# A three-layer graph attention kernel: transposes of h by DMA, attention rows in PSUM, the skip connection as an accumulating DMA

## The chip, the cores and the metric

The kernel runs on one core of one Trainium2 chip. The metric is the device time in microseconds (us) of one execution; one launch computes all 128 graphs.

## The reference, cut to what matters

The input x is [128 graphs, 128 nodes, 256 features] in float32, adj is [128, 128, 128] in int32. All weights are float32; there are three layers.

```python
h = relu(layernorm(x))                       # over the 256 features, no affine part
mask = adj + eye > 0
for l in range(3):
    si, sj = h @ attn_w[l, :256], h @ attn_w[l, 256:]
    scores = leaky_relu(si[:, :, None] + sj[:, None, :] + attn_b[l], slope 0.2)
    attn = softmax(where(mask, scores, -inf), axis=-1)
    agg = einsum('bij,bjd->bid', attn, h)
    h1 = layernorm(h + agg) * g1[l] + beta1[l]
    ff = gelu(h1 @ W1[l] + b1[l]) @ W2[l] + b2[l]      # 256 -> 1024 -> 256
    h = layernorm(h1 + ff) * g2[l] + beta2[l]
out = x + h
```

## The kernel before, in words

**Tiling.** Four graphs make a group (T = 4), nodes on the 128 partitions; there are 32 groups and so 96 items (a group in one layer). Items are numbered s: eight groups go through layer 0, then the same eight through layer 1, then layer 2, and then come the next eight, so that one round has 24 slots (PER = 24, RING = 8). Precision is kept with split operands: a float32 value becomes two float16 values, hi and lo, and each product is three matmuls (hi by hi, lo by hi, hi by lo).

**Stages of an item.** Dot products with the two attention vectors (L613, L616 on VectorE). s_j is spread over rows by TensorE (L404) into the PSUM bank p_att. Scores, row maxima (L631, L637). Leaky ReLU and exponentials on ScalarE (L507 to L513). The probabilities are transposed by TensorE (L410) into p_att again, split into hi and lo (L518, L660), and aggregate with the split X (L422). Residual, statistics (L650, L579, L584 to L587), the inverse deviation on GpSimd (L786, L788), normalization on ScalarE into norm1 (L488). norm1 is transposed by TensorE, 8 blocks of 128x128 in float32 (L432), and split into hT_hi (ScalarE, L534) and hT_lo (VectorE, L665). GpSimd makes the residual h_res (L798, L800). Then for each of eight chunks c of the hidden width: first product (L366), GELU and its split (L478, L483, L572), second product (L380), which adds up in PSUM. Residual of the feed-forward into res2 (L675, feed_residual), statistics, inverse deviation, norm2 (L812, norm_feed), layer output (L826, L828). In the last layer the input is added from a second copy, x_again, which SyncE has loaded (L835), and the result is stored.

**Order.** There is no planner. Each engine runs a function slot(r, s), written out by hand, that interleaves parts of up to eight items; within it the chunks c = 0 to 7 order everything. In slot s TensorE, VectorE and ScalarE work on the chunks of item s. At c = 0 TensorE aggregates for item s + 1, at c = 4 it transposes norm1 of s + 1 and spreads s_j of s + 2, at c = 7 it transposes the probabilities of s + 2. VectorE does feed_residual of item s - 1 at c = 2; this waits until norm2 of item s - 2 is complete, because res2 and norm2 have one buffer each:

```python
            def feed_residual(r, s):
                dve.wait_ge(ff_done, total(r, s, C, C))
                dve.wait_ge(h_res_steps, total(r, s, 2, 2))
                if later(r, s):
                    dve.wait_ge(norm2_ready, total(r, s - 1, 4, 4))
```

Every engine executes its own list in order, and semaphores tie the engines together. The two tensors p_pair (each two PSUM banks) are used in turn: item s gathers its second product in p_pair[s % 2], and before that the transposes of norm1 and the aggregate of s + 1 use the one that is free. All DMAs of before are issued by SyncE, in one queue.

Of the kernel before, what the change touches and what calls it, by code (L numbers as in the profile page):

```python
# [35 lines left out]
P = 128  # L36
B, N, D = 128, 128, 256
L = 3
# [15 lines left out]
FIRST_SLOT = -4  # L54
# [38 lines left out]
def x_total(r, s, n):  # L93

    v = 4 * s + RING * (s // PER) + max(0, s % PER - (PER - RING)) + n
    return (4 * PER + RING) * r + v if isinstance(r, int) else r * (4 * PER + RING) + v


def group_of(r, s):
    return RING * (r + s // PER) + s % RING  # L100

# [32 lines left out]
def gnn_kernel(nc, x, adj, attn_w, attn_b, W1, b1, W2, b2, g1, beta1, g2, beta2, out):  # L134
    with ExitStack() as ctx:
# [37 lines left out]
        x_again = [w2_f32[:, i * T:(i + 1) * T, :] for i in range(2)]  # L173
# [19 lines left out]
        hT_hi = [sb(f"hT_hi{i}", [P, KD, TN], F16) for i in range(2)]  # L193
        hT_lo = [sb(f"hT_lo{i}", [P, KD, TN], F16) for i in range(2)]
# [16 lines left out]
        p_att = ps("p_att", [P, T, N])  # L211

# [7 lines left out]
        def nT_banks(s):  # L220
            return p_pair[s % 2][:].rearrange("p (k u) d -> p k (u d)", k=KD)

        def agg_banks(s):
            return p_pair[(s - 1) % 2]

# [9 lines left out]
        x_again_loaded = [sem(f"x_again_loaded{i}") for i in range(2)]  # L235
        stored = [sem(f"stored{i}") for i in range(2)]
        mask_steps = sem("mask_steps")
        x0_ready = sem("x0_ready")
        dots_ready = sem("dots_ready")
# [15 lines left out]
        nT_psum = sem("nT_psum")  # L255
# [25 lines left out]
        def _(sp):  # L281
# [20 lines left out]
            def load_again(g):  # L302
                sp.dma_start(x_again[g % 2], graphs(x, g)).then_inc(x_again_loaded[g % 2], 16)

            def store(r, s):
                g = group_of(r, s)
                sp.wait_ge(x_steps, x_total(r, s, 5))
                sp.dma_start(graphs(out, g), y_out[g % 2]).then_inc(stored[g % 2], 16)
                if g + 2 < G:
                    load_again(g + 2)  # L310
            def slot(r, s):
                if is_item(r, s + 2) and layer_of(s + 2) == 0 and group_of(r, s + 2) + 2 < G:
                    sp.wait_ge(x0_ready, group_total(r, s + 2, 4, 4))
                    load_x(group_of(r, s + 2) + 2)
# [13 lines left out]
                if (r, s) == (0, 5):  # L328
                    sp.wait_ge(w_lo_ready, 4 * L)
                    load_again(0)  # L330
                    load_again(1)
# [21 lines left out]
        def _(pe):  # L353
            def hidden(r, s, c):

                l, i = layer_of(s), s % 2
                if c == 0:
                    pe.wait_ge(hT_hi_ready, total(r, s, 1, 1))
# [26 lines left out]
            def fold_bias(l):  # L385
# [3 lines left out]
                for c in range(C):  # L389
                    for k in range(KD):  # L390
                        mm = pe.matmul(p_att[:, 0, c:c + 1], w1_f32[:, k, c * P:(c + 1) * P], beta1_col[:, l, k:k + 1],
# [3 lines left out]
            def spread_sj(r, s):  # L395

                pe.wait_ge(dots_ready, total(r, s, 8, 8))
                if later(r, s):
                    pe.wait_ge(pT_lo_ready, total(r, s - 1, 1, 1))
                if isinstance(r, int) and r == 0 and s in FOLD_AT:  # L400
                    fold_bias(FOLD_AT[s])
                    pe.wait_ge(bias_ready, FOLD_AT[s] + 1)
                for t in range(T):
                    mm = pe.transpose(p_att[:, t, :], s_j[s % RING][:, t:t + 1].broadcast_to([P, P]), ident[:])  # L404
                mm.then_inc(sj_rows_ready, 1)

            def transpose_probs(r, s):
                pe.wait_ge(probs_ready, total(r, s, 4, 4))
                for t in range(T):
                    mm = pe.transpose(p_att[:, t, :], probs[:, t, :], ident[:])  # L410
                mm.then_inc(pT_psum, 1)

            def aggregate(r, s):
# [3 lines left out]
                if later(r, s):  # L417
                    pe.wait_ge(hT_lo_ready, total(r, s - 1, 1, 1))
# [6 lines left out]

            def transpose_norm1(r, s):
                if later(r, s, 2):
                    pe.wait_ge(res2_ready, total(r, s - 2, 2, 2))
                pe.wait_ge(norm1_ready, total(r, s, 4, 4))
                for k in range(KD):  # L430
                    for t in range(T):
                        mm = pe.transpose(nT_banks(s)[:, k, t * N:(t + 1) * N],  # L432
                                          norm1[:, t, k * P:(k + 1) * P], ident[:])
                mm.then_inc(nT_psum, 1)

            def slot(r, s):
                for c in range(C):
# [15 lines left out]
                    if c == 4 and is_item(r, s + 1):  # L453
                        transpose_norm1(r, s + 1)
# [9 lines left out]
        def _(act):  # L464
# [32 lines left out]
            def norm_attention(r, s):  # L497
                act.wait_ge(rstd_ready[1], total(r, s, 2, 2))
                if later(r, s):
                    act.wait_ge(nT_psum, total(r, s - 1, 1, 1))  # L500
# [15 lines left out]
            def copy_probs(r, s):  # L516
                act.wait_ge(pT_psum, total(r, s, 1, 1))
                act.activation(pT_hi[:], p_att[:].rearrange("p t n -> p (t n)"), ACT.Copy).then_inc(pT_hi_ready, 1)  # L518
# [10 lines left out]
            def high_hT(r, s):  # L529

                act.wait_ge(nT_psum, total(r, s, 1, 1))
                if later(r, s, 2):
                    act.wait_ge(hid_psum, total(r, s - 2, C, C))
                act.activation(hT_hi[s % 2][:], nT_banks(s), ACT.Copy).then_inc(hT_hi_ready, 1)  # L534

            def slot(r, s):
                if isinstance(r, int) and r == 0 and s in (0, 3):
                    act.wait_ge(bias_ready, 1 if s == 0 else L)
                for c in range(C):
# [6 lines left out]
                    if c == 3 and is_item(r, s + 2):  # L546
                        high_X(r, s + 2)
                    if c == 4 and is_item(r, s + 1):
                        high_hT(r, s + 1)
# [4 lines left out]
                    if c == 7 and is_item(r, s + 3) and layer_of(s + 3) == 0:  # L554
                        norm_input(r, s + 3)
# [4 lines left out]
        def _(dve):  # L560
# [44 lines left out]
            def dot_products(r, s, pair):  # L605

                l, q = layer_of(s), s % RING
                if l == 0:
# [3 lines left out]
                for t in (2 * pair, 2 * pair + 1):  # L612
                    dve.tensor_tensor_reduce(out=dots[:, 2 * t, :], in0=X[q][:, t, :], in1=attn_rows[:, l, 0, :], scale=1.0,  # L613
                                             scalar=attn_b_col[:, l:l + 1], op0=ALU.mult, op1=ALU.add,
                                             accum_out=s_i[q][:, t:t + 1]).then_inc(dots_ready, 1)
                    dve.tensor_tensor_reduce(out=dots[:, 2 * t + 1, :], in0=X[q][:, t, :], in1=attn_rows[:, l, 1, :], scale=1.0,  # L616
# [3 lines left out]
            def add_bias(l):  # L620
                dve.wait_ge(bias_psum, l + 1)
                dve.tensor_tensor(b1_eff[:, l, :], p_att[:, 0, 0:C], b1_col[:, l, :], ALU.add).then_inc(bias_ready, 1)

            def add_scores(r, s):
# [5 lines left out]
                for t in range(T):  # L630
                    dve.scalar_tensor_tensor(out=scores[:, t, :], in0=p_att[:, t, :], scalar=s_i[q][:, t:t + 1],  # L631
# [26 lines left out]
            def low_probs(r, s):  # L658
                dve.wait_ge(pT_hi_ready, total(r, s, 1, 1))
                dve.tensor_tensor(pT_lo[:], p_att[:].rearrange("p t n -> p (t n)"), pT_hi[:],  # L660
                                  ALU.subtract).then_inc(pT_lo_ready, 1)

            def split_hT(r, s):
                dve.wait_ge(hT_hi_ready, total(r, s, 1, 1))
                dve.tensor_tensor(hT_lo[s % 2][:], nT_banks(s), hT_hi[s % 2][:], ALU.subtract).then_inc(hT_lo_ready, 1)  # L665
# [17 lines left out]
            def last_output(r, s):  # L683
# [4 lines left out]
                dve.wait_ge(x_again_loaded[s % 2], 16 * G // 2)  # L688
# [8 lines left out]
                dve.wait_ge(x_steps, x_total(r, s, 4))  # L697
                dve.tensor_tensor(y, y, x_again[s % 2], ALU.add).then_inc(x_steps, 1)

            def slot(r, s):  # L700
                starts = is_item(r, s + 4) and layer_of(s + 4) == 0

                late = isinstance(r, int) and (r, s) == (0, -3)
                if isinstance(r, int) and (r, s) == (0, -2):
# [3 lines left out]
                for c in range(C):  # L708
# [5 lines left out]
                    if c == 6 and starts and not late:  # L714
                        dve.wait_ge(stat_steps[0], group_total(r, s + 4, 10, 4))
                    if isinstance(r, int) and (r, s, c) == (0, -2, 3):
# [12 lines left out]
                    if isinstance(r, int) and (r, s, c) == (0, -2, 2):  # L729
                        input_statistics(0, 1)  # L730
                    if isinstance(r, int) and (r, s, c) == (0, -2, 3):
                        aggregates(0, group_total(0, 1, 10, 8))
                    if c == 3 and is_item(r, s - 1):
                        feed_statistics(r, s - 1)
                    if c == 4 and isinstance(r, int) and r == 0 and s + 2 in FOLD_AT:
                        add_bias(FOLD_AT[s + 2])
# [5 lines left out]
                    if c == 5 and is_item(r, s + 1):  # L742
                        split_hT(r, s + 1)
                    if c == 5 and starts and not late:
                        input_statistics(r, s + 4)
                    if c == 6 and is_item(r, s + 2):
                        low_probs(r, s + 2)
                    if c == 6 and starts and not late:
                        aggregates(0, group_total(r, s + 4, 10, 8))
                    if c == 6 and is_item(r, s + 2):  # L750
                        row_sums(r, s + 2)
                    if c == 6 and starts:
# [15 lines left out]
        def _(pool):  # L768
# [21 lines left out]
            def h_residual(r, s):  # L790
# [3 lines left out]
                if is_item(r, s + 1):  # L794
                    pool.wait_ge(dots_ready, total(r, s + 1, 8, 8))
# [82 lines left out]
```

## Time and profile before

| quantity | value |
|---|---|
| median of 3 runs (lowest to highest) | 2402.95 us (2402.5 to 2403.74) |
| profiled execution: its own time | 2401.22 us |
| its span | 2399.4 us |
| mean granted TensorE clock | 0.995 of full speed |
| busy, TensorE matmul | 2333.0 us (97%), 16608 instructions |
| busy, VectorE | 1869.7 us (78%), 5974 instructions |
| busy, ScalarE | 1892.0 us (79%), 3498 instructions |
| busy, GpSimd | 1698.2 us (71%), 1543 instructions |
| the DMA queue of SyncE | 77184 packets, 67.79 MB, 9.1% of 16 engines' span |

The span runs from the first to the last instruction. The profiled execution lies 1.7 us below the median of the three runs. Busy time is the union of an engine's instructions. A matmul's end is modelled, so on TensorE the distance between starts says more than the durations: a 128x256 float16 matmul has 273 ns beside it, and they follow each other every 0.11 us.

### The profile page before, as it was taken

Reading aid. Unit: us, or ns where it says so; the run is one execution under the profiler, and the core shown is the slowest. Engines: PE = TensorE matmul, PEld = TensorE weight load, DVE = VectorE, ACT = ScalarE, POOL = GpSimd, SP = SyncE. Lnnn points to the kernel's source line nnn. Section 1 sums busy time; section 2 is a strip of 40 time slices with the busy share of each in tenths; the row PEclk is TensorE's granted clock in tenths of the full one; section 3 lists DMA queues with packets and bytes.
Section 4 is the critical chain, followed back from the end, with each engine's and each line's share of the span. In section 5 each row is a group of like instructions: output and inputs, shape, how many; then the busy total and the mean of one; then the engine's idle time right before and its main releaser. Section 6 shows DMA issues by size and latency. Waiting matters only on the chain.

```text
span 2399.4 us, 47629 instructions
## 1 busy us (share of the span) xinstructions
PE 2333.0 (97%) x16608; PEld 1649.3 (69%) x16608; DVE 1869.7 (78%) x5974; ACT 1892.0 (79%) x3498; POOL 1698.2 (71%) x1543
## 2 busy tenths in 40 slices
PE   3999999999999999999999999999999999999997
PEld 2667777776666777777666777777766677777775
DVE  6887777777888777777888787878788877787874
ACT  4878787878888878787888877778788887878783
POOL 3567676768887666667887767676878776767686
PEclk9999999999999999999999999999999999999998
DMA  5200000001211000001121000000121100000012
GB/s 162 87 28 27 1 1 2 1 19 41 93 62 36 1 1 1 1 1 36 54 78 60 23 2 1 1 1 2 53 67 63 41 2 1 1 1 1 19 42 65
DMA packets 77421, 70.83 MB, mean 30 GB/s; under 512 B 7040, under 2 KB 75648, under 8 KB 77184
## 3 DMA queue, kind: packets, MB, share of 16 engines
q1 hardware_dynamic: 77184, 67.79, 9.1%
q8 instruction: 134, 2.20, 0.4%
q14 instruction: 103, 0.84, 0.1%
HBM read 51.01 MB, written 16.78 MB: 28 GB/s over the span
## 4 chain that ended last, share of the span: by engine, by line
PE 66%; POOL 16%; DVE 11%; ACT 3%; issue 2%; POOLq 0%; DVEq 0%
PE p_pair L380 29%; PE p_hid L366 28%; PE p_pair L422 4%; PE p_pair L432 2%; POOL rstd L786 2%; DVE dots L613 2%; DVE g_lo L572 2%; POOL w_f L835 2%; POOL h_res L798 2%; POOL h_res L800 2%; POOL norm L812 2%; DVE res L675 2%; POOL w_f L828 2%; POOL X_lo L804 2%; POOL w_f L826 2%
## 5 line engine op out<-in xcount | busy, mean ns | idle before, releaser
L380 PE MATMUL p_pair<-w_hi,g_hi 128*128 128x256 f16 x3072 | 837.6, 273 | 0.0
L380 PE MATMUL p_pair<-w_lo,g_hi 128*128 128x256 f16 x3072 | 837.6, 273 | 0.0
L380 PE MATMUL p_pair<-w_hi,g_lo 128*128 128x256 f16 x3072 | 837.5, 273 | 0.0
L572 DVE TENSOR_TENSOR g_lo<-p_hid,g_hi 128x512 f16<-128x512 f32 x768 | 528.6, 688 | 396.2 <-ACT g_hi L483 389.7
L478 ACT ACTIVATE p_hid<-p_hid,b_eff 128x512 f32<-128x512 f32 x768 | 504.5, 657 | 316.9 <-PE p_hid L366 315.7
L798 POOL TENSOR_TENSOR h_res<-norm,g_rows 128x1024 f32<-128x1024 f32 x96 | 227.7, 2372 | 384.0 <-DVE res L675 377.3
L483 ACT ACTIVATE g_hi<-p_hid 128x512 f16<-128x512 f32 x768 | 458.6, 597 | 24.4
L366 PE MATMUL p_hid<-hT_hi,w_hi 128*128 128x512 f16 x1536 | 458.2, 380 | 1.5 <-DVE g_lo L572 1.4
L366 PE MATMUL p_hid<-hT_hi,w_lo 128*128 128x512 f16 x1536 | 458.3, 380 | 0.0
L366 PE MATMUL p_hid<-hT_lo,w_hi 128*128 128x512 f16 x1536 | 457.9, 380 | 0.0
L786 POOL TENSOR_TENSOR rstd<-var_eps,minus_half 128x4 f32<-128x4 f32 x224 | 242.2, 1081 | 259.0 <-DVE minus_mean L587 253.7
L380 PEld LDWEIGHTS p_pair<-w_lo,g_hi 128*128 128x128 f16 x3072 | 300.7, 98 | 106.5 <-issue 0.3
L380 PEld LDWEIGHTS p_pair<-w_hi,g_hi 128*128 128x128 f16 x3072 | 300.7, 98 | 105.6 <-issue 0.4
L380 PEld LDWEIGHTS p_pair<-w_hi,g_lo 128*128 128x128 f16 x3072 | 300.7, 98 | 34.8
L488 ACT ACTIVATE norm<-res,shift,rstd 128x256 f32<-128x256 f32 x384 | 199.4, 590 | 97.6 <-POOL shift L788 97.6
L366 PEld LDWEIGHTS p_hid<-hT_hi,w_lo 128*128 128x128 f16 x1536 | 150.6, 98 | 182.2 <-issue 1.7
L366 PEld LDWEIGHTS p_hid<-hT_lo,w_hi 128*128 128x128 f16 x1536 | 150.6, 98 | 182.2 <-issue 1.7
L579 DVE BATCH_NORM_STATS2 bn<-res 128x6 f32<-128x256 f32 x768 | 269.5, 416 | 3.3
L800 POOL TENSOR_TENSOR h_res<-h_res,res_rows 128x1024 f32<-128x1024 f32 x96 | 227.0, 2364 | 7.5
L812 POOL TENSOR_SCALAR norm<-res,rstd,shift 128x256 f32<-128x256 f32 x384 | 207.5, 555 | 10.0
L650 DVE SCALAR_TENSOR_TENSOR res<-p_pair,row_inv,X 128x256 f32<-128x256 f32 x384 | 159.1, 477 | 67.6 <-PE p_pair L422 67.5
L804 POOL TENSOR_TENSOR X_lo<-X,X_hi 128x1024 f16<-128x1024 f32 x96 | 204.6, 2132 | 0.0
(68 smaller groups left out, 3658.5 us busy)
## 6 DMA issues: line engine op xcount, KB each, us to landing
x_in<-in_x SPq DMA_DIRECT2D x32, 512.0 KB, 4.1
w_f<-in_x SPq DMA_DIRECT2D x32, 512.0 KB, 5.8
out<-w_f SPq DMA_DIRECT2D x32, 512.0 KB, 4.2
adj_in<-in_adj SPq DMA_DIRECT2D x32, 256.0 KB, 4.5
w_f<-in_L_gnn_W SPq DMA_DIRECT2D x6, 1024.0 KB, 6.1
attn_rows<-in_L_gnn_attn_w SPq DMA_DIRECT2D x1, 768.0 KB, 5.9
g_rows<-in_L_gnn_g SPq DMA_DIRECT2D x2, 384.0 KB, 7.5
b_rows<-in_L_gnn_b SPq DMA_DIRECT2D x1, 384.0 KB, 6.7
```

The costliest lines, as they stand in the source:

```text
L366: mm = pe.matmul(p_hid[in_ring(s, c, PF_RING)][:], w[l][:, k, cols], h[i][:, k, :], start=(n == 0), stop=(n == 3 * KD - 1))
L380: mm = pe.matmul(ff_banks(s)[:, t, :], g[i][:, nodes], w[l][:, c, :], start=(c == 0 and t % 2 == 0 and n == 0), stop=(c == C - 1 and n == ...
L478: act.activation(p_hid[k][:], p_hid[k][:], ACT.Gelu, bias=b1_eff[:, l, c:c + 1], scale=1.0 / WSCALE).then_inc(gelu_ready, 1)
L483: act.activation(g_hi[i][:], p_hid[k][:], ACT.Copy).then_inc(g_hi_ready, 1)
L488: act.activation(dst[:, t, :], src[:, t, :], func, bias=shift[n][s % 2][:, t:t + 1], scale=rstd[n][s % 2][:, t:t + 1]).then_inc(done, 1)
L572: dve.tensor_tensor(g_lo[i][:], p_hid[k][:], g_hi[i][:], ALU.subtract).then_inc(g_lo_ready, 1)
L579: dve.bn_stats(bn[n][:, t, :], src[:, t, :]).then_inc(stat_steps[n], 1)
L786: pool.tensor_tensor(rstd[n][s % 2][:], var_eps[n][:], minus_half[:], ALU.pow).then_inc(rstd_ready[n], 1)
L798: pool.tensor_tensor(h_res[i][:], norm1[:], rows(g1_rows, l, T), ALU.mult).then_inc(h_res_steps, 1)
L800: pool.tensor_tensor(h_res[i][:], h_res[i][:], rows(res_rows, l, T), ALU.add).then_inc(h_res_steps, 1)
L804: pool.tensor_tensor(X_lo[:], X[s % RING][:], X_hi[:], ALU.subtract).then_inc(X_lo_ready, 1)
L812: pool.tensor_scalar(norm2[:, t, :], res2[:, t, :], rstd[2][s % 2][:, t:t + 1], shift[2][s % 2][:, t:t + 1], ALU.mult, ALU.add).then_inc(n ...
```

## The change

1. **Transposes of h.** The eight float32 transposes of norm1 on TensorE (L432) go, and so do the two splits out of PSUM (L534, L665). In their place ScalarE copies norm1 to float16 (h_hi, high_h, at c = 3; high_X moves to c = 4), GpSimd subtracts (low_h, h_lo), and SyncE issues two DMA transposes SBUF to SBUF for each item, each of [128, 1024] float16 (turn_h). The first product reads hT in the order [t, k].
2. **GpSimd's order.** Before: inverse deviation of s + 1, h_residual of s + 1, low_X of s + 2, inverse deviation, norm_feed and (after the skip connection and the input's inverse deviation) layer_output of s - 1. After: inverse deviation of s + 1; inverse deviation, norm_feed and layer_output of s - 2; low_h of s + 1; low_X; h_residual; the input's inverse deviation; the skip connection of s - 2.
3. **Rows in PSUM.** p_att goes. s_j and the transposed probabilities use the two banks of the p_pair that the aggregate will use. The free bank takes the two attention vectors of a layer (p_rows), copied once for eight items by VectorE; the dot products read them there. They move from c = 1 (item s + 2) to c = 5 (item s + 3). The input's statistics move one slot earlier, to c = 1 and c = 2.
4. **Skip connection.** x_again, its loads and the additions (L835, L698) go. GpSimd issues a DMA from x that accumulates onto y_out, and the store waits for it.

The core of the diff (the changes of buffers' declarations, the prologue's slots and the renaming of banks are left out):

```diff
@@ sync @@
+            def turn_h(r, s):
+                i = s % 2
+                if later(r, s, 2):
+                    sp.wait_ge(hid_psum, total(r, s - 2, C, C))
+                for h, hT, made, turned in ((h_hi, hT_hi, h_hi_ready, hT_hi_ready), (h_lo, hT_lo, h_lo_ready, hT_lo_ready)):
+                    sp.wait_ge(made, total(r, s, 1, 1))
+                    sp.dma_start_transpose(hT[i][:].rearrange("p t k n -> p (t k) n"),
+                                           h[:].rearrange("p t d -> p (t d)")).then_inc(turned, 16)
...
                 if is_item(r, s - 3) and layer_of(s - 3) == L - 1:
                     store(r, s - 3)
+                if is_item(r, s + 1):
+                    turn_h(r, s + 1)
@@ tensor @@
                 if c == 0:
-                    pe.wait_ge(hT_hi_ready, total(r, s, 1, 1))
+                    pe.wait_ge(hT_hi_ready, total(r, s, 16, 16))
...
                     if c == 0 and n == 2 * KD:
-                        pe.wait_ge(hT_lo_ready, total(r, s, 1, 1))
-                    mm = pe.matmul(p_hid[in_ring(s, c, PF_RING)][:], w[l][:, k, cols], h[i][:, k, :],
+                        pe.wait_ge(hT_lo_ready, total(r, s, 16, 16))
+                    mm = pe.matmul(p_hid[in_ring(s, c, PF_RING)][:], w[l][:, k, cols], h[i][:, :, k, :],
                                    start=(n == 0), stop=(n == 3 * KD - 1))
...
             def spread_sj(r, s):
                 pe.wait_ge(dots_ready, total(r, s, 8, 8))
-                if later(r, s):
-                    pe.wait_ge(pT_lo_ready, total(r, s - 1, 1, 1))
+                if later(r, s, 3):
+                    pe.wait_ge(res2_ready, total(r, s - 3, 2, 2))
...
-                    if c == 4 and is_item(r, s + 1):
-                        transpose_norm1(r, s + 1)
@@ scalar @@
-            def high_hT(r, s):
-                act.wait_ge(nT_psum, total(r, s, 1, 1))
...
+            def high_h(r, s):
+                act.wait_ge(norm1_ready, total(r, s, 4, 4))
+                if later(r, s):
+                    act.wait_ge(hT_hi_ready, total(r, s - 1, 16, 16))
+                act.activation(h_hi[:], norm1[:], ACT.Copy).then_inc(h_hi_ready, 1)
@@ vector @@
+                if q == 0 and pair == 0:
+                    dve.tensor_copy(p_rows[:], attn_rows[:, l]).then_inc(rows_ready, 1)
+                    dve.wait_ge(rows_ready, rows_total(r, s))
...
-                    if c == 1 and is_item(r, s + 2):
-                        if is_item(r, s - 2):
-                            dve.wait_ge(x_steps, x_total(r, s - 2, 4))
-                        dot_products(r, s + 2, 0)
-                        dot_products(r, s + 2, 1)
...
+                    if c == 1 and starts and not late:
+                        input_statistics(r, s + 5)
+                    if c == 2 and starts and not late:
+                        aggregates(0, group_total(r, s + 5, 10, 8))
...
-                    if c == 5 and is_item(r, s + 1):
-                        split_hT(r, s + 1)
...
+                    if c == 5 and is_item(r, s + 3):
+                        dot_products(r, s + 3, 0)
+                        dot_products(r, s + 3, 1)
@@ gpsimd @@
             def h_residual(r, s):
                 pool.wait_ge(norm1_ready, total(r, s, 4, 4))
-                if is_item(r, s + 1):
-                    pool.wait_ge(dots_ready, total(r, s + 1, 8, 8))
...
+            def low_h(r, s):
+                pool.wait_ge(h_hi_ready, total(r, s, 1, 1))
+                if later(r, s):
+                    pool.wait_ge(hT_lo_ready, total(r, s - 1, 16, 16))
+                pool.tensor_tensor(h_lo[:], norm1[:], h_hi[:], ALU.subtract).then_inc(h_lo_ready, 1)
...
                 pool.wait_ge(x_steps, x_total(r, s, 4))
-                pool.wait_ge(x_again_loaded[i], lane_total(r, s - 2 * RING))
-                pool.tensor_tensor(y_out[i], y_out[i], x_again[i], ALU.add).then_inc(x_steps, 1)
+                g = group_of(r, s)
+                pool.dma_start(y_out[i], x.rearrange("(g t) n d -> n g t d", t=T)[:, g],
+                               accum_op=ALU.add).then_inc(skipped[i], 16)
...
                 if is_item(r, s + 1):
                     inverse_deviation(s + 1, 1, total(r, s + 1, 10, 10), total(r, s + 1, 2, 1))
-                    h_residual(r, s + 1)
+                if is_item(r, s - 2):
+                    inverse_deviation(s - 2, 2, total(r, s - 2, 10, 10), total(r, s - 2, 2, 1))
+                    norm_feed(r, s - 2)
+                    layer_output(r, s - 2)
+                if is_item(r, s + 1):
+                    low_h(r, s + 1)
                 if is_item(r, s + 2):
                     low_X(r, s + 2)
-                if is_item(r, s - 1):
-                    inverse_deviation(s - 1, 2, total(r, s - 1, 10, 10), total(r, s - 1, 2, 1))
-                    norm_feed(r, s - 1)
+                if is_item(r, s + 1):
+                    h_residual(r, s + 1)
+                if is_item(r, s + 5) and layer_of(s + 5) == 0:
+                    inverse_deviation(s + 5, 0, group_total(r, s + 5, 10, 10), group_total(r, s + 5, 2, 1))
                 if is_item(r, s - 2) and layer_of(s - 2) == L - 1:
                     skip_connection(r, s - 2)
...
```

## Rows read from the trace of the kernel before

**Rows 1.** The page, part 1: busy time and share of the span, by engine.

```profile
PE 2333.0 (97%) x16608; PEld 1649.3 (69%) x16608; DVE 1869.7 (78%) x5974; ACT 1892.0 (79%) x3498; POOL 1698.2 (71%) x1543
```

**Rows 2.** The waits: engine and line, releaser, us in total, times, longest.

```profile
PEld p_att L410 <- ACT probs L513: 42.0, 95, 4.8
```

**Rows 3.** Timeline of TensorE over one slot: start, us, instruction, count.

```profile
963.36 0.27 PE L422 MATMUL p_pair<-X_hi,pT_hi 128*128 128x256 f16 x1
...
975.09 1.04 PE L432 MATMUL p_pair<-ident,norm 128*128 128x128 f32 x8
975.97 0.60 PE L404 MATMUL p_att<-ident,s_j 128*128 128x128 f32 x4
...
982.91 0.60 PE L410 MATMUL p_att<-ident,probs 128*128 128x128 f32 x4
...
985.52 0.59 PE L366 MATMUL p_hid<-hT_lo,w_hi 128*128 128x512 f16 x2
...
987.26 0.27 PE L422 MATMUL p_pair<-X_hi,pT_hi 128*128 128x256 f16 x1
```

**Rows 4.** Timeline of GpSimd in the same stretch.

```profile
981.67 1.01 POOL L786 TENSOR_TENSOR rstd<-var_eps,minus_half 128x4 f32<-128x4 f32 x1
...
983.07 2.16 POOL L812 TENSOR_SCALAR norm<-res,rstd,shift 128x256 f32<-128x256 f32 x4
985.19 1.27 POOL L826 TENSOR_TENSOR X<-norm,g_rows 128x512 f32<-128x512 f32 x1
...
989.11 1.28 POOL L828 TENSOR_TENSOR X<-X,beta_rows 128x512 f32<-128x512 f32 x1
993.22 1.02 POOL L786 TENSOR_TENSOR rstd<-var_eps,minus_half 128x4 f32<-128x4 f32 x1 [2.83 <-DVE minus_mean L587]
...
998.72 2.36 POOL L798 TENSOR_TENSOR h_res<-norm,g_rows 128x1024 f32<-128x1024 f32 x1 [4.18 <-DVE res L675]
...
1003.47 2.13 POOL L804 TENSOR_TENSOR X_lo<-X,X_hi 128x1024 f16<-128x1024 f32 x1
```

**Rows 5.** Timeline of VectorE in the same stretch.

```profile
985.40 0.69 DVE L572 TENSOR_TENSOR g_lo<-p_hid,g_hi 128x512 f16<-128x512 f32 x1 [4.09 <-ACT g_hi L483]
...
988.77 1.66 DVE L650 SCALAR_TENSOR_TENSOR res<-p_pair,row_inv,X 128x256 f32<-128x256 f32 x4 [1.00 <-PE p_pair L422]
...
992.51 0.37 DVE L584 BATCH_NORM_AGGREGATE mv<-bn 128x2 f32<-128x6 f32 x4
...
997.26 1.29 DVE L675 SCALAR_TENSOR_TENSOR res<-p_pair,h_res 128x512 f32<-128x512 f32 x2
...
1004.00 1.22 DVE L665 TENSOR_TENSOR hT_lo<-p_pair,hT_hi 128x1024 f16<-128x1024 f32 x1
```

**Rows 6.** Timeline of VectorE in one of the longer slots.

```profile
635.26 1.28 DVE L675 SCALAR_TENSOR_TENSOR res<-p_pair,h_res 128x512 f32<-128x512 f32 x2
```

**Rows 7.** Timeline of TensorE in the same slot.

```profile
644.70 0.66 PE L410 MATMUL p_att<-ident,probs 128*128 128x128 f32 x4
```

**Rows 8.** DMA: the queue (packets, MB, share), issues (count, KB, us to landing).

```profile
q1 hardware_dynamic: 77184, 67.79, 9.1%
...
x_in<-in_x SPq DMA_DIRECT2D x32, 512.0 KB, 4.1
...
adj_in<-in_adj SPq DMA_DIRECT2D x32, 256.0 KB, 4.5
...
beta_rows<-in_L_gnn_beta SPq DMA_DIRECT2D x1, 384.0 KB, 8.2
```

**Rows 9.** Busy time in one stretch: PE, PEld, DVE, ACT, POOL, granted clock, DMA.

```profile
70.00:75.00 5.00, 4.74 (x25) 3.13 (x25) 1.98 (x6) 0.40 (x1) 2.19 (x2) 0.66 0.00 0
```

**Rows 10.** Timeline of TensorE: first and last of 89 such rows, one a slot.

```profile
205.41 0.60 PE L404 MATMUL p_att<-ident,s_j 128*128 128x128 f32 x4
...
2325.97 0.60 PE L404 MATMUL p_att<-ident,s_j 128*128 128x128 f32 x4
```

More of the change, by code:

```diff
@@ L93, in x_total, with rows_total @@
 def x_total(r, s, n):
-    v = 4 * s + RING * (s // PER) + max(0, s % PER - (PER - RING)) + n
-    return (4 * PER + RING) * r + v if isinstance(r, int) else r * (4 * PER + RING) + v
+    return 4 * (PER * r + s) + n
 def group_of(r, s):
     return RING * (r + s // PER) + s % RING
+def rows_total(r, s):
+    return L * (r + s // PER) + layer_of(s) + 1
 def is_item(r, s):
@@ L192, in gnn_kernel @@
         h_res = [sb(f"h_res{i}", [P, T, D]) for i in range(2)]
-        hT_hi = [sb(f"hT_hi{i}", [P, KD, TN], F16) for i in range(2)]
-        hT_lo = [sb(f"hT_lo{i}", [P, KD, TN], F16) for i in range(2)]
+        h_hi, h_lo = sb("h_hi", [P, T, D], F16), sb("h_lo", [P, T, D], F16)
+        hT_hi = [sb(f"hT_hi{i}", [P, T, KD, N], F16) for i in range(2)]
+        hT_lo = [sb(f"hT_lo{i}", [P, T, KD, N], F16) for i in range(2)]
         g_hi = [sb(f"g_hi{i}", [P, TN], F16) for i in range(GS_RING)]
@@ L234, in gnn_kernel @@
         adj_loaded = [sem(f"adj_loaded{i}") for i in range(2)]
-        x_again_loaded = [sem(f"x_again_loaded{i}") for i in range(2)]
+        skipped = [sem(f"skipped{i}") for i in range(2)]
         stored = [sem(f"stored{i}") for i in range(2)]
@@ L383, in feed, with fold_bias @@
                 mm.then_inc(ff_done, 1)
-            def fold_bias(l):
+            def fold_bias(l, bank):
                 pe.wait_ge(w_dma[0], 16 * (l + 1))
@@ L424, in aggregate @@
                 mm.then_inc(agg_ready, 1)
[L426 to L434, printed above, removed]
             def slot(r, s):
@@ L630, in add_scores @@
                 for t in range(T):
-                    dve.scalar_tensor_tensor(out=scores[:, t, :], in0=p_att[:, t, :], scalar=s_i[q][:, t:t + 1],
+                    dve.scalar_tensor_tensor(out=scores[:, t, :], in0=sj_bank(s)[:, t, :], scalar=s_i[q][:, t:t + 1],
                                              in1=mask[q][:, t, :], op0=ALU.add, op1=ALU.add).then_inc(score_steps, 1)
@@ L696, in last_output @@
                     dve.tensor_tensor(y[:, pair, :], y[:, pair, :], beta2_pair, ALU.add).then_inc(x_steps, 1)
-                dve.wait_ge(x_steps, x_total(r, s, 4))
-                dve.tensor_tensor(y, y, x_again[s % 2], ALU.add).then_inc(x_steps, 1)
             def slot(r, s):
-                starts = is_item(r, s + 4) and layer_of(s + 4) == 0
-                late = isinstance(r, int) and (r, s) == (0, -3)
-                if isinstance(r, int) and (r, s) == (0, -2):
+                starts = is_item(r, s + 5) and layer_of(s + 5) == 0
+                late = isinstance(r, int) and (r, s) == (0, -4)
+                if isinstance(r, int) and (r, s) == (0, -3):
                     dve.wait_ge(attn_dma, 2 * 16)
@@ L713, in slot @@
                         dve.wait_ge(stat_steps[2], total(r, s - 1, 10, 4))
-                    if c == 6 and starts and not late:
-                        dve.wait_ge(stat_steps[0], group_total(r, s + 4, 10, 4))
-                    if isinstance(r, int) and (r, s, c) == (0, -2, 3):
+                    if c == 2 and starts and not late:
+                        dve.wait_ge(stat_steps[0], group_total(r, s + 5, 10, 4))
+                    if isinstance(r, int) and (r, s, c) == (0, -3, 1):
                         dve.wait_ge(stat_steps[0], group_total(0, 1, 10, 4))
@@ L741, in slot @@
                         aggregates(2, total(r, s - 1, 10, 8))
-                    if c == 5 and is_item(r, s + 1):
-                        split_hT(r, s + 1)
-                    if c == 5 and starts and not late:
-                        input_statistics(r, s + 4)
+                    if c == 5 and is_item(r, s + 3):
+                        dot_products(r, s + 3, 0)
+                        dot_products(r, s + 3, 1)
                     if c == 6 and is_item(r, s + 2):
                         low_probs(r, s + 2)
-                    if c == 6 and starts and not late:
-                        aggregates(0, group_total(r, s + 4, 10, 8))
                     if c == 6 and is_item(r, s + 2):
                         row_sums(r, s + 2)
-                    if c == 6 and starts:
+                    if c == 6 and is_item(r, s + 4) and layer_of(s + 4) == 0:
                         make_mask(r, s + 4)
```

90 lines of the change are left out of this document (39 added, 51 removed).

## The prediction

> **What bounds the kernel now.** The page's busy shares come first: TensorE is busy 97% of the span, the others 71 to 79% [rows 1]. So I read TensorE's timeline over one slot. The aggregate of one item starts at 963.36 and that of the next at 987.26 [rows 3]: a slot takes 23.90 us, and its matmuls follow each other without a gap, so that slot is TensorE's own work. The reader should then ask how near the next limit is, since taking work off TensorE gives time only down to it. The waits show it: in 95 of 96 items TensorE's weight loads for the transposes of the probabilities wait for ScalarE's exponentials, 0.44 us each (42.0 / 95) [rows 2]. That chain (VectorE's feed_residual, scores, row maxima, exponentials, transposes, aggregate) has practically no slack. Over the steady part, 88 slots take 2325.97 - 205.41 = 2120.6 us, 24.10 each [rows 10]: some slots are longer than 23.90.
>
> **TensorE's part.** The eight transposes of norm1 go: from 975.09 to 975.97, 0.88 us a slot [rows 3]. That leaves 23.02 us of TensorE work. Spreading s_j and transposing the probabilities keep their count, only their bank changes, and cost the same. If nothing else came last, the slot would be 23.02. I now look for what comes last, counting from A, the start of an item's aggregate (987.26 [rows 3]). Every loop below goes from A to the next item's A.
>
> **Loop one: norm2, feed_residual, exponentials.** The statistics of the aggregate reach GpSimd at 993.22, A + 5.96 [rows 4, 5]; nothing in this stretch is changed, and both engines are tight in it. Then GpSimd's new order applies. After the inverse deviation of s + 1 (1.40, as from 981.67 to 983.07 [rows 4]) it does that of s - 2 (1.40 again) and norm2 of s - 2 (2.16 [rows 4]): norm2 is complete at A + 10.92. Before, this had been done one slot earlier. VectorE's feed_residual of s - 1, at c = 2, waits for exactly this, since res2 has one buffer. With the crossing between engines (0.07, as statistics to rstd) it starts at A + 10.99, 998.25 in this slot, where before it started at 997.26 [rows 5]. The dot products, which had filled VectorE until then, are gone from there, but the wait takes their place, and what is queued behind it on VectorE is g_lo of c = 3, the statistics, the scores and the row maxima, and behind these the exponentials. How long is that tail? In a slot where TensorE did wait, feed_residual starts at 635.26 and the transposes of the probabilities at 644.70, 9.44 us later [rows 6, 7]; the operations in between are kept. From there to the aggregate it is TensorE's fixed 4.35 (982.91 to 987.26 [rows 3]). The loop is 10.99 + 9.44 + 4.35 = 24.78 us. That is 0.88 longer than the slot of before, and 1.76 longer than TensorE's new work: the whole gain is spent on a wait. In the first slots of a group (30 of the 88), aggregates of the input's statistics now stand at c = 2 behind feed_residual, inside this tail: about 0.6 (992.51 to the next engine's start at 993.22, without the crossing [rows 4, 5]). The mean is 24.78 + 0.6 x 30/88 = 24.98.
>
> **Loop two: low_h and the DMA.** GpSimd goes on from A + 10.92 with the layer output, 5.20 (985.19 to the end of the row at 989.11 [rows 4]), and only then low_h, priced as low_X with the same shape and types, 2.13 [rows 4]: h_lo is there at A + 18.25. h_hi is not late: norm1's time is unchanged and ScalarE's copy costs what the copy out of PSUM did. The DMA transpose of h_lo takes d. TensorE needs hT_lo at the third pair of c = 0, 985.52, 1.74 before the aggregate [rows 3]. The loop is 18.25 + d + 1.74 = 20.0 + d. It exceeds loop one from d = 4.8 on, or 5.0 against its mean.
>
> **The size of d.** No row shows a DMA transpose. Loads of 512 KB and 256 KB land after 4.1 and 4.5 [rows 8], the slowest row after 8.2. A packet occupies an engine 0.091 x 2399.4 x 16 / 77184 = 0.045 us [rows 8]. The load of x has rows of 1 KB, 512 packets, 32 for each of 16 engines, 1.45 us; so 2.65 of its 4.1 is fixed. A transpose of [128, 1024] float16 has 1024 row pieces of 256 B if each 128x128 block is turned for itself: 64 an engine, 2.9 us, d = 5.5. If it goes by whole rows of 2 KB it is 8 an engine, 0.36 us, d = 3.0. So d is 3.0 to 8.2; I take 5.5, since turning blocks must break the rows. Both transposes then fit in a slot: the first is issued about 6.7 us before the second, with d below that. Loop two is 25.5 us.
>
> A rule speaks for less: the Trainium skill (Advanced Engine Details and Errata, X-Bar Transpose (TRN2)) holds that transposing DMAs are as fast as regular ones. By it d would be about the 4.5 of the 256 KB load [rows 8], and loop one would decide. No run here shows it; it is one of the rivals.
>
> **The other edits.** GpSimd has in a slot 1.40 + 1.40 + 2.16 + 5.20 + 2.13 + 2.13 + 4.75 (h_residual, 998.72 to 1003.47 [rows 4]) = 19.2, and 1.40 more where a group starts; 20.6 of 25.5. The subtraction of x_again (2.35, as one pass of h_residual [rows 4]) goes, but it had cover. The accumulating DMA costs GpSimd an issue that no row shows: from 0 to 4.9 it is covered, above it would add the rest in 32 slots. Nothing reads its result but the store, which stands a slot later on SyncE ahead of the next h_hi transpose, with about 3 us to spare. I take 0; its far end, 8.2 as the slowest DMA row, is 3.3 x 32 = 106 us. Dot products from PSUM: 3.0 us at c = 5 in place of hT_lo's 1.22, before a VectorE idle stretch of 4.09 [rows 5]; some 2.3 us of cover remain, so faster or slower reads give nothing. The copy of the vectors, twelve times, fits there too. ScalarE keeps its work. Outside the steady part: the first six slots are partly bound by the weights and take about 1 us more each, the fill gets one transpose in its chain (5.5), and the end swaps an addition for a DMA ahead of the store (about +2, from 0 to 8.2). Together +13.
>
> **Sum.** 88 x (25.5 - 24.10) = +123, with +13 it is +136 on the profiled 2401.2: 2537. The median of before is 1.7 above that, so 2539 us.
>
> **Rivals.**
> (a) d is under 5.0, loop one decides: 88 x (24.98 - 24.10) + 13 = +90, 2493 us. For it: plain loads of this size land in 4.1 to 4.5. Against: the pieces are short.
> (b) The DMA transposes are far slower, 8.2 or more: the slot is 28.2, +361 + 13, 2777 us, and above about 7 they would also queue behind each other. For it: no row bounds the rate.
> (c) TensorE's clock falls. In 70 to 75 the clock was granted at 0.66, so part of the stretch at 1.2 GHz, after TensorE had done 128x1 matmuls and waits for 4 us [rows 9]. A gap of 2.5 us in each slot, right ahead of the 1.74 us that lie on loop two, could do it: matmuls there at 1.2 GHz add 1.7, and 88 x 1.7 = 150 makes 2689. The Trainium skill (TensorE: Matmul & The Clock Gate, HAM oscillation) describes such a return to the low clock at every wait for data. Against: the longer slots of before have gaps too and keep 2.4 GHz.
> (d) Faster: GpSimd gets through the inverse deviation and norm2 quicker than in the rows, since VectorE reads a shared operand from PSUM and less from SBUF meanwhile. It decides if loop one falls under 23.9, that is if 4.96 us shrink by 0.9, and d is under 3.9; at the full 1.76, TensorE bounds at 23.02: 88 x (23.02 - 24.10) + 13 = -82, 2321 us. Against: these rows were taken with VectorE partly idle.
> (e) No change, the two meet near 24.0.
>
> **Chances.** The forecast 0.40, (a) 0.27, (b) 0.09, (c) 0.08, (d) 0.11, (e) 0.05. A measurement can tell 0.2% from no change. Faster 0.12, the same 0.03, slower 0.85. The range: from 2455, below (a), to 2750, which takes in (c) and nearly (b). The forecast's own range, d from 5 to 7, is 2490 to 2675.
>
> **What would show it.** In the profile after: 23.0 us of TensorE work in slots of 25 to 26; TensorE waiting at L366 of c = 0 for the DMA of h_lo, about once per item; low_h ending near A + 18.3 and feed_residual waiting for norm2 at A + 11; DMAs to hT_lo landing after 5 to 6 us. If instead the wait is for the exponentials and landings are under 5, it is (a). Slots below 23.9 would make the loops wrong, above all the claim that norm2 of s - 2 holds back feed_residual.

## The result and the profile after

| | median | lowest to highest | ratio to before, 95% interval |
|---|---|---|---|
| before | 2403.18 us (4 runs) | 2402.5 to 2403.74 | |
| after | 2491.07 us (4 runs) | 2487.34 to 2492.38 | 1.0368 [1.0355, 1.0381] |

The change makes the kernel 88 us slower. The time lies in the range and on the side forecast, but 48 us below the forecast of 2539: it is that of rival (a), 2493. The head of the page of after (span; busy time and share by engine) shows where the work went: TensorE's busy time is 55 us shorter than in [rows 1], and it is busy 91% of a longer span instead of 97%.

```profile
span 2490.5 us, 46242 instructions
...
PE 2278.2 (91%) x15840; PEld 1561.2 (63%) x15840; DVE 1786.3 (72%) x5889; ACT 1894.5 (76%) x3498; POOL 1858.3 (75%) x1640
```

The waits of after (engine and line, releaser, us in total, times, longest) name the reason. The first one, VectorE's feed_residual waiting for norm2, did not exist before; the second, 42.0 us in [rows 2], has nearly quadrupled; the third is the wait that my forecast had put first.

```profile
DVE res L671 <- POOL norm L806: 295.5, 93, 3.6
...
PEld p_pair L420 <- ACT probs L511: 160.4, 95, 12.1
...
PE p_hid L376 <- DMA hT_lo<-h_lo: 0.6, 1, 0.6
```

One slot in the timelines of after answers to [rows 3 to 5]. TensorE first (start, us, instruction, count, idle before and its releaser): a slot is 992.26 - 967.50 = 24.76 us, and TensorE stands still twice, 0.89 ahead of the transposed probabilities and 0.45 ahead of s_j.

```profile
967.50 0.62 PE L414 MATMUL p_pair<-ident,s_j 128*128 128x128 f32 x4 [0.45 <-DVE res L671]
...
975.51 0.66 PE L420 MATMUL p_pair<-ident,probs 128*128 128x128 f32 x4 [0.89 <-ACT probs L511]
...
979.92 0.27 PE L432 MATMUL p_pair<-X_hi,pT_hi 128*128 128x256 f16 x1
...
992.26 0.62 PE L414 MATMUL p_pair<-ident,s_j 128*128 128x128 f32 x4 [0.45 <-DVE res L671]
```

GpSimd in that slot:

```profile
985.88 1.02 POOL L776 TENSOR_TENSOR rstd<-var_eps,minus_half 128x4 f32<-128x4 f32 x1 [5.87 <-DVE minus_mean L584]
...
987.13 1.01 POOL L776 TENSOR_TENSOR rstd<-var_eps,minus_half 128x4 f32<-128x4 f32 x1
...
988.53 2.16 POOL L806 TENSOR_SCALAR norm<-res,rstd,shift 128x256 f32<-128x256 f32 x4
```

VectorE in that slot:

```profile
990.83 1.29 DVE L671 SCALAR_TENSOR_TENSOR res<-p_pair,h_res 128x512 f32<-128x512 f32 x2 [3.49 <-POOL norm L806]
```

The reader is to see the loop. The aggregate starts at 979.92; GpSimd gets the statistics 5.96 later; norm2 of item s - 2 ends at 990.69; feed_residual starts at 990.83, after 3.49 us in which VectorE had nothing to do, though GpSimd itself had been idle for 5.87 us until the statistics came, and did norm2 only behind them.

The DMA rows answer to [rows 8] (queue: packets, MB, share; issues: count, KB where known, us to landing):

```profile
q1 hardware_dynamic: 263040, 101.37, 17.5%
...
hT_lo<-h_lo SPq DMA_TRANSPOSE x96, 3.1
```

### The profile page after: what moved, and what is told of

It reads as the page before. It is cut to its first block, busy times and chain, and to the rows that moved or that the text cites. A ratio compares the mean times of both kernels' runs of the same rounds, so it can differ in the third digit from the quotient of the medians.

```text
span 2490.5 us, 46242 instructions
## 1 busy us (share of the span) xinstructions
PE 2278.2 (91%) x15840; PEld 1561.2 (63%) x15840; DVE 1786.3 (72%) x5889; ACT 1894.5 (76%) x3498; POOL 1858.3 (75%) x1640
## 2 busy tenths in 40 slices
DMA packets 280169, 121.11 MB, mean 49 GB/s; under 512 B 209792, under 2 KB 278400, under 8 KB 279936
## 4 chain that ended last, share of the span: by engine, by line
DVE 36%; PE 24%; POOL 17%; ACT 13%; issue 8%; DMA 1%; SPq 0%; DVEq 0%; POOLq 0%; ACTq 0%
PE p_pair L390 10%; DVE bn L576 10%; POOL norm L806 8%; POOL rstd L776 7%; DVE res L650 6%; PE p_hid L376 6%; ACT probs L511 5%; ACT L511 5%; PE p_pair L432 5%; DVE res L671 5%; DVE g_lo L569 5%; DVE scores L631 4%; DVE row_top L637 3%; PE p_pair L420 2%; ACT leaky L506 2%
## 5 line engine op out<-in xcount | busy, mean ns | idle before, releaser
L671 DVE SCALAR_TENSOR_TENSOR res<-p_pair,h_res 128x512 f32<-128x512 f32 x192 | 123.6, 686 | 298.7 <-POOL norm L806 295.5
L794 POOL TENSOR_TENSOR h_lo<-norm,h_hi 128x1024 f16<-128x1024 f32 x96 | 205.5, 2140 | 11.9 <-ACT h_hi L531 11.9
```

The lines of the kernel that those rows point to most:

```text
L671: dve.scalar_tensor_tensor(out=res2[:, pair, :], in0=ff_banks(s)[:, pair, :], scalar=1.0 / WSCALE, in1=h_res[s % 2][:, pair, :], op0=ALU.m ...
```

## The experiments

Theory: the loop over norm2 of s - 2, feed_residual and the exponentials sets the slot (loop one). Rival 1: the DMA transposes set it. Rival 2: the accumulating DMA's work on GpSimd, or the dot products from PSUM. The runs of before beside these had a median of 2401.5 us.

**norm2 first.** The kernel after with this edit (in the edits shown here, "..." stands for arguments and lines left out):

```diff
+                if is_item(r, s - 2):
+                    inverse_deviation(s - 2, 2, ...)
+                    norm_feed(r, s - 2)
                 if is_item(r, s + 1):
                     inverse_deviation(s + 1, 1, ...)
                 if is_item(r, s - 2):
-                    inverse_deviation(s - 2, 2, ...)
-                    norm_feed(r, s - 2)
                     layer_output(r, s - 2)
```

> The kernel after, with one edit: GpSimd does the inverse deviation and norm2 of item s - 2 ahead of the inverse deviation of s + 1, in its idle stretch. Theory (the wait of feed_residual for norm2 closes the loop of 24.8 us): the wait goes, the next limits are TensorE's own 23.0 us and ScalarE's chain from shift to exponentials, about 23.1; slots of 23.1, 88 x (23.1 - 24.9) = -160, about 2330 us. Rival 1 (the DMA transposes, their latency or their traffic in SBUF, make the slot longer): no change, near 2490. Rival 2 (the accumulating DMA's work on GpSimd or the dot products from PSUM): no change, near 2490.

Measured: 2351.71 us (2349.43 to 2353.56), ratio 0.9789 [0.9774, 0.9804]. No instruction was added or taken away, and it is 139 us under after. Both rivals had said 2490. The wait of VectorE for norm2 is gone; TensorE's timeline gives slots of 23.38 to 23.39 (not 23.1):

```profile
985.72 0.60 PE L414 MATMUL p_pair<-ident,s_j 128*128 128x128 f32 x4
...
1009.11 0.60 PE L414 MATMUL p_pair<-ident,s_j 128*128 128x128 f32 x4
```

**res2 in two buffers**, GpSimd's order kept:

```diff
-        res2 = sb("res2", [P, T, D])
+        res2 = [sb(f"res2_{i}", [P, T, D]) for i in range(2)]
...
-                if later(r, s):
-                    dve.wait_ge(norm2_ready, total(r, s - 1, 4, 4))
+                if later(r, s, 2):
+                    dve.wait_ge(norm2_ready, total(r, s - 2, 4, 4))
```

> The kernel after with res2 in two buffers, so that feed_residual waits for norm2 of one item earlier; GpSimd's order is kept (aggregates of these statistics wait for the inverse deviation of the item before, since var_eps has one buffer, and the bias rows borrow the last X buffer in the prologue, for space). Theory: the same loop is cut at another place, slots of 23.1 and about 2330 us, equal to the run with norm2 first within 10 us. Rivals 1 and 2: near 2490. If it is the order of GpSimd's queue itself and not the buffer that costs, this one stays near 2490 and only the reordered one gains.

Measured: 2385.3 us (2384.5 to 2385.59), ratio 0.9929 [0.9914, 0.9944]. 106 us under after: cutting the loop at the buffer frees most slots too (23.39), so it is the wait and not the queue's order as such. It missed the 10 us: in the slots where groups end and start at once a slot took 24.9. There one instruction of VectorE, the addition that makes the mask (the trace shows it as one on uint16; it reads two operands from SBUF), took a median of 2546 ns here against 661 in after (instructions of that line: duration ns min/median/max):

```profile
L597 DVE CUSTOM_DVE_ANT_0 adj_in<-eye_i,adj_in x32: 659/2546/2571, 6.6 to 1895.4; 128x1024 uint16<-128x1024 uint16 x32
```

It now falls beside GpSimd's h_residual. The mean slot is 23.81 against 23.44 with norm2 first, so the slots make up 33 of the 34 us between the two runs; that the mask's addition is what lengthens them is read from the rows, and no run takes it away. Why such an instruction grows there is the subject of the run with rows in SBUF, below.

**h_lo transposed twice**, to test loop two:

```diff
                     sp.wait_ge(made, total(r, s, 1, 1))
+                    if made is h_lo_ready:
+                        sp.dma_start_transpose(hT[i]..., h[:]...).then_inc(turned_once, 16)
+                        sp.wait_ge(turned_once, total(r, s, 16, 16))
```

> The kernel after with the transpose of h_lo done twice, one after the other (SyncE waits for the first to land, then issues the second). Theory: loop two is 20.0 + d, with d = 3.1 it has 1.7 us of slack under 24.8; with d of about 6.2 to 6.6 it becomes 26.2 to 26.6 and decides: slots + 1.4 to 1.8, 2490 + 88 x 1.5 = about 2620 us. If loop two is not as I worked it out (more slack): no change, 2490. Rival 1 (the transposes already decide by their latency): each slot longer by the whole 3.1 or more, 2765 us.

Measured: 2596.37 us (2592.73 to 2597.51), ratio 1.0805 [1.0789, 1.0821]. The slots take 25.97, 1.2 more than in after, where the added DMA takes 3.1. So 1.9 us of it were covered by the slack of loop two, the loop over low_h and the DMA (the forecast's 20.0 + 3.1 leaves 1.7 under 24.78). TensorE now does wait for the DMA:

```profile
1115.62 0.60 PE L381 MATMUL p_hid<-hT_lo,w_hi 128*128 128x512 f16 x2 [1.02 <-DMA hT_lo<-h_lo]
```

The 2620 expected was 24 us too much; low_h ends 0.2 sooner in the loop than worked out.

**The order alone**, on the kernel before, with no DMA transpose in it. The edit also brings the accumulating DMA, and it drops two waits of before: that of the dot products for the layer output, and that of h_residual for the dot products:

```diff
-                        if is_item(r, s - 2):
-                            dve.wait_ge(x_steps, x_total(r, s - 2, 4))
                         dot_products(r, s + 2, 0)
...
-                if is_item(r, s + 1):
-                    pool.wait_ge(dots_ready, total(r, s + 1, 8, 8))
...
                     inverse_deviation(s + 1, 1, ...)
-                    h_residual(r, s + 1)
+                if is_item(r, s - 2):
+                    inverse_deviation(s - 2, 2, ...)
+                    norm_feed(r, s - 2)
+                    layer_output(r, s - 2)
                 if is_item(r, s + 2):
                     low_X(r, s + 2)
-                if is_item(r, s - 1):
-                    inverse_deviation(s - 1, 2, ...)
-                    norm_feed(r, s - 1)
+                if is_item(r, s + 1):
+                    h_residual(r, s + 1)
...
```

> The kernel before (transposes on TensorE, rows in SBUF) with GpSimd's new order alone: norm2 and layer output of item s - 2 behind the inverse deviation of s + 1, h_residual at the end; the skip connection as an accumulating DMA, and without the two waits that tied the dot products to h_residual and to the layer output. Theory: the loop over norm2, feed_residual and exponentials is 24.8 here too, so about 2480 us with no DMA transpose in the kernel. Rival 1 (the DMA transposes) and the PSUM half of rival 2: it stays at 2385 to 2403.

Measured: 2537.44 us (2536.82 to 2539.34), ratio 1.0565 [1.0548, 1.0583]. The loss is there, and larger, without one DMA transpose; rival 1 is out. The slot is 25.44, 0.66 above the 24.78 expected. The timeline of GpSimd shows where that comes from, norm2 taking 2.55 in place of 2.16 (and the second inverse deviation 0.25 longer), while VectorE does the dot products from SBUF. So, as an estimate, some 77 of the 136 us (88 x 0.88) are the loop, and some 58 (88 x 0.66) are these longer rows, now that the dropped waits no longer keep the two apart; the accumulating DMA alone costs nothing (see the skip connection alone, below):

```profile
1024.94 2.55 POOL L796 TENSOR_SCALAR norm<-res,rstd,shift 128x256 f32<-128x256 f32 x4
```

**The attention vectors in SBUF again**, in the kernel after:

```diff
-                if q == 0 and pair == 0:
-                    dve.tensor_copy(p_rows[:], attn_rows[:, l]).then_inc(rows_ready, 1)
-                    dve.wait_ge(rows_ready, rows_total(r, s))
...
-                    dve.tensor_tensor_reduce(..., in1=p_rows[:, 0, :], ...)
+                    dve.tensor_tensor_reduce(..., in1=attn_rows[:, l, 0, :], ...)
```

> The kernel after with the two attention vectors read from SBUF again (no copy to PSUM); all else kept. Theory: the dot products at c = 5 lie in VectorE's idle stretch before g_lo of c = 6, so there is no change, 2490 within 5 us. Rival 2 (reads from PSUM are dearer, or the copy costs): 2480 or less. Rival 3 (the rows in PSUM help GpSimd's or VectorE's access to SBUF): 2500 or more.

Measured: 2879.32 us (2875.75 to 2882.71), ratio 1.1992 [1.1974, 1.201]. I had expected no change; undoing this part costs 388 us, the largest effect of the study. In the timeline of VectorE the second dot product of an item takes 2.34 us and the third and fourth 2.56 each; the other five keep 0.41 to 0.66:

```profile
997.41 2.34 DVE L613 CUSTOM_DVE_ANT_0 dots<-X,attn_rows 128x256 bf16<-128x256 f32 x1
...
999.68 2.56 DVE L610 CUSTOM_DVE_ANT_0 dots<-X,attn_rows,attn_b_col 128x256 bf16<-128x256 f32 x1
...
1002.17 2.56 DVE L613 CUSTOM_DVE_ANT_0 dots<-X,attn_rows 128x256 bf16<-128x256 f32 x1
```

GpSimd at the same time has three instructions and then nothing:

```profile
997.16 2.30 POOL L795 TENSOR_TENSOR X_lo<-X,X_hi 128x1024 f16<-128x1024 f32 x1
999.43 2.53 POOL L783 TENSOR_TENSOR h_res<-norm,g_rows 128x1024 f32<-128x1024 f32 x1
1002.04 2.41 POOL L785 TENSOR_TENSOR h_res<-h_res,res_rows 128x1024 f32<-128x1024 f32 x1
```

Each long dot product ends 0.28 to 0.29 us after the GpSimd instruction beside it (GpSimd's own rows are up to 0.2 longer than in after). VectorE is held up here where it reads both operands from SBUF, and not where one comes from PSUM: in after, under the same GpSimd work, the dot products take 0.47 and 0.41:

```profile
972.80 0.47 DVE L613 CUSTOM_DVE_ANT_0 dots<-X,p_rows,attn_b_col 128x256 bf16<-128x256 f32 x1
```

The Trainium skill (SBUF — State Buffer, Who interferes with whom) has the rule: a VectorE instruction with two SBUF inputs contends with a GpSimd instruction that reads SBUF, and one with a single SBUF input, outside the two-port modes, does not. The trace agrees: 2.56 us against 0.47.

The eight dot products together take some 6.4 us more than in after, of which VectorE's idle time of 2.25 us behind them covers a part; the mean slot is 29.24, 4.3 longer. A part of this is TensorE's clock. The aggregate now comes after 3.40 us without work, and its matmuls take 0.42 us in place of 0.27 and follow each other every 0.21 us in place of 0.11, as at the lower of the two levels (1.2 and 2.4 GHz); the clock granted from 1005 to 1010 is 0.71, and 0.935 over the span, against 0.990 in after.

```profile
1007.50 0.39 PE L432 MATMUL p_pair<-X_hi,pT_hi 128*128 128x256 f16 x1 [3.40 <-DVE pT_lo L657]
```

From its first to its last matmul start the aggregate takes 1.91 us as the mean of the steady part, against 1.21 where the clock stays high, so an estimate for the clock is 88 x 0.70 = 62 of the 388 us.

The kernel before has waits between dot products, layer output and h_residual that keep the two apart in time; that they stood there for this reason is argued, not shown. The run with the order alone drops them, and there GpSimd's norm2 grows.

**The skip connection alone**, on the kernel before:

```diff
-                pool.tensor_tensor(y_out[i], y_out[i], x_again[i], ALU.add).then_inc(x_steps, 1)
+                pool.dma_start(y_out[i], x...[:, g], accum_op=ALU.add).then_inc(skipped[i], 16)
```

> The kernel before with the fourth part of the change alone: the skip connection as an accumulating DMA, no second copies. Theory: it frees 2.3 us of GpSimd in 32 slots, the issue costs it 1.3; of this only the some 24 slots that were longer than 23.9 (by 0.5 to 0.8) can show: -10 to -18, and about +2 to +4 at the end, so 2388 to 2396 us. Rival (the issue on GpSimd or the traffic of the DMA costs more than the addition): 2410 or more.

Measured: 2401.98 us (10 runs, 2399.68 to 2404.82), ratio 1.0002 [0.9992, 1.0011]: no change, the gain of 10 to 18 us is not there. The longer slots went from 24.67 to 24.57 only. The issue takes 1.27 us of GpSimd, and then it waits 0.93 for statistics of VectorE that it had not waited for before; so 0.1 of the 2.35 us reached the chain.

```profile
644.22 1.27 POOL L823 DMA_DIRECT2D w_f<-in_x  x1
646.41 1.47 POOL L774 TENSOR_TENSOR rstd<-var_eps,minus_half 128x4 f32<-128x4 f32 x1 [0.93 <-DVE minus_mean L578]
```

**Statistics moved**, on norm2 first; they now stand behind feed_residual and their aggregates behind the dot products:

```diff
-                    if c == 1 and starts and not late:
+                    if c == 2 and starts and not late:
                         input_statistics(r, s + 5)
-                    if c == 2 and starts and not late:
+                    if c == 5 and starts and not late:
                         aggregates(0, group_total(r, s + 5, 10, 8))
```

> The kernel with norm2 first, and the input's statistics at c = 2 behind feed_residual, their aggregates at c = 5 behind the dot products, both in idle stretches of VectorE and 3 us later after the load of x. Theory: the slots of 23.5 to 24.7 beside the usual 23.38 come from statistics that wait for x; they go, about -8: 2343 us. Otherwise no change, 2351.

Measured: 2347.44 us (2346.43 to 2348.54), ratio 0.9777 [0.9762, 0.9791]. 4 us less than norm2 first, half of what was expected; nearly all slots are 23.38 now.

**Scores first**, on statistics moved:

```diff
+                    if c == 4 and is_item(r, s + 2):
+                        add_scores(r, s + 2)
+                        row_maxima(r, s + 2)
                     if is_item(r, s):
                         hidden(r, s, c)
...
-                    if c == 4 and is_item(r, s + 2):
-                        add_scores(r, s + 2)
-                        row_maxima(r, s + 2)
```

> As the run with the statistics moved, and at c = 4 VectorE does scores and row maxima ahead of g_lo. Theory: slots of 23.38 are set by g_hi of c = 4, g_lo, scores, row maxima, exponentials; with g_lo off that chain ScalarE's own work (0.28 us of idle ahead of the exponentials goes) and TensorE's 23.02 are next: slots of 23.1, 88 x 0.28 = -25, about 2318 us. Rival: TensorE itself already sets 23.38 and nothing changes, 2343.

Measured: 2311.98 us (2311.71 to 2313.01), ratio 0.9629 [0.9613, 0.9645], the best of all: 35 us under the run before it, 90 under the kernel before as measured beside it. Its slots are 23.02 to 23.03, which is to the last digit TensorE's work as worked out before. In the busy time of one stretch (length, then PE, PEld, DVE, ACT, POOL, granted clock, DMA share, GB/s) TensorE shows no free time:

```profile
1000.00:1200.00 200.00, 200.00 (x1430) 140.33 (x1429) 163.82 (x547) 170.46 (x316) 173.41 (x157) 1.00 0.32 70
```

## Why the prediction was right or wrong

**The direction, and loop one: right.** I had worked out 24.78 us for the slot and 0.6 more where a group starts. Measured: 24.77, and 25.34. feed_residual starts 10.91 after the aggregate (990.83 - 979.92; worked out: 10.99), and the cause is shown by three runs: reordering alone gives 139 us back, a second buffer 106, and the order in the kernel before makes it slower by 136, of which some 77 are this loop.

**TensorE's part: right.** 23.02 us was worked out and is what the last run shows.

**The size of d: wrong, and with it the likeliest case.** I took 5.5 us for the DMA transpose, "since turning blocks must break the rows", and so made loop two the longer one. It lands after 3.1. The step with the pieces held: packets under 512 B rose from 7040 to 209792, which is 1056 for each of 192 transposes, about the 1024 pieces of 256 B. What failed is the price of a piece and the fixed part, both taken from plain loads [rows 8]. The run with the skip connection alone has neither transposes nor second copies, and its queue holds 60288 packets and 6.7% of 2397.9 us. (So a load of 512 KB is 528 packets and not the 512 of my sum.) The transposes' share is (0.175 x 2490.5 - 0.067 x 2397.9) x 16 = 4403 us of engine time for 202752 packets: 0.022 us each, not 0.045. By this estimate the 66 packets of an engine are 1.4 us, and 1.7 of the 3.1 are fixed, not the 2.65 taken from a load out of HBM. With d, the time of a DMA transpose, at 3.1, loop two is 23.1, 1.7 under loop one; the doubled transpose found 1.9. The rule of the Trainium skill (Advanced Engine Details and Errata, X-Bar Transpose (TRN2)), that a transposing DMA is as fast as a regular one, came nearer than my sum: 3.1 here, against 4.2 for the load of 512 KB and 7.4 for that of 256 KB in after, which share the queue with other work.

**The sum.** The 88 slots take 2413.26 - 219.88 = 2193.4 us, 24.92 each; against the 2120.6 of before that is +72.8. Fill and end give +18.3, where +13 had been put: the first s_j row of the steady part stands at 219.88, 14.5 later than in [rows 10]. That the time falls on rival (a)'s 2493 within 2 us is in part luck: its steady part, +77, was about 5 too much (24 slots were longer, not 30), and its +13 about 5 too little.

**The other edits.** The issue of the accumulating DMA had cover, as said (1.34 us on GpSimd). The dot products had cover too (2.25 us of idle time are left behind them, 2.3 in my sum), but what I left out is what they cost with both operands in SBUF: in their new place, beside GpSimd's long instructions, that is 388 us, so the rows in PSUM are what makes this place usable. Rival (d) had the mechanism and the wrong place for it. The rule of the Trainium skill (SBUF — State Buffer, Who interferes with whom) on two SBUF inputs, which I had not brought to this sum, points at it.

**The clock, rival (c): did not come in after.** The gaps of 0.89 and 0.45 us a slot leave the granted clock at 1.00 in the steady part. The mean over the profiled span went from 0.995 to 0.990, but the four executions of after lie between 0.990 and 0.995 themselves. The mechanism is real in this kernel all the same: with the rows in SBUF, TensorE stands still for 3.0 to 3.4 us ahead of the aggregate, and in 79 of 89 slots its clock is down for a part of it. No run has the gap of 2.5 us that rival (c) supposed.

What stays open: norm2 first gave slots of 23.38 where I expected 23.1. The last run shows that g_lo of c = 4 was in the chain; that ScalarE alone would have held it at 23.1 was not borne out, since it fell to 23.02.

## What to carry to other kernels

Taking work off the busiest engine gives time down to the next loop through the others, so work out the loops of the new order, not only the engine's sum: here 0.88 us a slot were to gain, and one position in an idle engine's queue turned that into a loss of 0.9. When an order is rewritten, put first what another engine waits for, and let the engine's idle time fall behind it. A wait of before that looks needless may keep two engines from reading SBUF at once; test that by itself before dropping it.

## What the runs showed of the hardware

A VectorE instruction with two operands in SBUF (the dot products, 128x256, and the uint16 addition of the mask) took 2.56 us in place of 0.47, and 2.55 in place of 0.66, beside GpSimd instructions of 2.4 us; with one operand in PSUM it kept 0.47. In the run with the order alone it was GpSimd that was slowed beside the same dot products (norm2 2.55 in place of 2.16), while they kept 0.48: which engine pays is not the same in both.

A DMA transpose of [128, 1024] float16, SBUF to SBUF, takes 1.23 us to issue on SyncE and lands a median of 3.1 us after (in after from 3.0 to 3.8 for h_lo, up to 5.0 for h_hi). An accumulating DMA of 512 KB issued on GpSimd occupies it for 1.3 us and lands after 5.9 to 7.8, as medians of the runs.

With the rows in SBUF, 3.40 us without work on TensorE were followed by matmuls every 0.21 us in place of 0.11 and a granted clock of 0.71 in the 5 us around them; gaps of 0.89 and 0.45 in after left it at 1.00.
